# Local attention stack on one core: scores as products over two whole heads, queries moved across partitions by DMA

## Chip, core and metric
One core of a Trainium2 chip runs the whole kernel. The metric is the device time of one execution in microseconds. PE is TensorE, DVE is VectorE, ACT is ScalarE, POOL is GpSimd, and SP is SyncE, which in this kernel issues every DMA. Where a view says SPq, DVEq or PEq, it means that engine's sequencer: what it issues or signals, as distinct from its arithmetic.

## What is computed
The program is a small transformer on x of shape (8, 512, 128): layer norm and attention with 16 heads of 8, then a stack of six layers of local attention with feed-forward, then a second attention block and a gated mix. The change is in the stack. Cut to what matters, one layer of it does this:

```python
q, k, v = split(x @ Wqkv)                 # 16 heads of 64, n = 512 positions
q = rope(l2norm(q) * qs) * scale
k = rope(l2norm(k) * ks) / scale
# windows of 32 positions; each window of queries sees its own and the previous window of keys
sim  = einsum('bhwie,bhwje->bhwij', q_windows, k_two_windows) * 8.0    # 32 x 64 per head and window
attn = softmax(where(mask, -max, sim))
out  = einsum('bhwij,bhwje->bhwie', attn, v_two_windows) @ Wo
x = out + x
x = geglu_ffn(layernorm(x)) + x
```

## The kernel before
Features lie on the 128 partitions and positions along the free axis. `local_stack` walks over 6 layers and, inside a layer, over the 8 sequences of the batch (`body`); a body has four units, `for c in range(NC)`, one for each group of four heads. That makes 6 x 8 x 4 = 192 units. All five engines run the same nest in their own order, and only semaphores tie them together. It is a software pipeline: in unit c the engines project the queries and keys of group c (PE L1021 and L1034), form sums of squares (L1047) and values (L1062), and at the same time work on earlier groups: the scores of group c-2 (L1070 to L1074), the normalised queries and keys `qn` and `kn` of group c-1 (DVE L954), and the product of probabilities with values of group c-3 (PE L1112). Unit c=2 also holds six products with Wo (L1011), and unit c=3 the residual, the layer norm and the feed-forward.

One half of each head lies in `qn[:, 0, :]` and the other in `qn[:, 1, :]`: head r of the group has 32 of its 64 dimensions on partitions 32r to 32r+31 of either half. Keys must not mix between heads when all 128 partitions are contracted, so the keys go by DMA into a block-diagonal tile: `kbd[i]` has four blocks of columns, one per head, and block r is zero outside the partitions of head r. SP issues eight DMAs per unit for that (L775), 32 partitions by 512 positions each:

```python
sp.wait_ge(S["kn_ready"], seen.next(S["kn_ready"]))
...
sp.dma_start(kbd[i][q, r, WIN:KC], kn[q, i, :]).then_inc(S["kbd_full"], 16)
```

The scores of one window are then two products, one per half, with 32 columns of queries as the stationary operand and 4 heads x 64 keys = 256 moving columns; the second accumulates onto the first. A product in float32 shows as two matmul records in the trace, so a unit has 2 banks x 16 products x 2 = 64 records of L1074. The additive mask enters each of the two PSUM banks first, as one bfloat16 product with an identity (L1070).

After the scores, DVE takes the row maximum (L941, tile `l_smax`), subtracts it (L943), later sums and inverts, POOL normalises (L801), and DVE transposes the probabilities in blocks of 32 (L903, tile `l_pt`). SP copies the result into the band `pbd` with eight more DMAs (L764, L767, L768). Before DVE may overwrite `pt`, it waits for `pt_free`, which SP gives at L759 in its own order, after the DMA issues of the unit before:

```python
sp.wait_ge(S["pbd_free"], seen.next(S["pbd_free"]))
sp.sem_inc(S["pt_free"], 1)
sp.wait_ge(S["pt_ready"], seen.next(S["pt_ready"]))
```

DVE's order in a unit is: rotation of the queries (L890), read of the sums of squares (L926), transpose (L903), inverse square root (L87 to L96), rotation of the keys (L890), maximum and subtraction (L941, L943), `qn`, `kn` (L954), sum and reciprocal (L959, L961). PE's order is L1021, L1034, L1047, L1062, scores, broadcast of the norms (L1085, needs the inverse square root), L1112. L1021 of the next unit needs the PSUM tile that L954 reads, so it starts when `kn` is done (semaphore at L956).

Of the kernel before, what the change touches and what calls it, by code (L numbers as in the profile page):

```python
# [15 lines left out]
D = 128  # L16
NB = 8
T = 512
# [16 lines left out]
WIN = 32  # L35
NC = 4
CH = H // NC
KC = T + WIN
# [610 lines left out]
def local_stack(nc, C, xs, A):  # L649
# [8 lines left out]
    with ExitStack() as ctx:  # L658
        def sb(n, shape, dt=F32):
            return ctx.enter_context(nc.sbuf_tensor(f"l_{n}", shape, dt))  # L660
# [18 lines left out]
        kbd = [sb(f"kbd{i}", [D, CH, KC]) for i in range(2)]  # L679
# [22 lines left out]
                 "qn_ready kn_ready kbd_full s_ready t_ready p_ready rec_ready pn_ready pt_ready pt_free pbd_free "  # L702
                 "va_ready pv_ready ot_ready wo_ready x_ready mean_ready centred fsq_ready bc_ready xng_ready "
                 "xnf_ready g_ready a_ready gelu_ready h_ready f_ready ffn_done step pstep init mask_full").split()
        S = {n: sem(n) for n in names}
# [24 lines left out]
        def _(sp):  # L730
# [18 lines left out]
            def body(par, l, start, b, prev):  # L749
# [6 lines left out]
                for c in range(NC):  # L756
# [13 lines left out]
                    if live(c, 1, b, prev):  # L770
                        sp.wait_ge(S["kn_ready"], seen.next(S["kn_ready"]))
                        for i in range(2):
                            for r in range(CH):
                                q = slice(32 * r, 32 * r + 32)
                                sp.dma_start(kbd[i][q, r, WIN:KC], kn[q, i, :]).then_inc(S["kbd_full"], 16)  # L775
# [209 lines left out]
        def _(pe):  # L985
# [5 lines left out]
            def body(par, l, start, b, prev):  # L991
# [23 lines left out]
                for c in range(NC):  # L1015
# [49 lines left out]
                    if live(c, 2, b, prev):  # L1065
                        claim(3, "r3_dve")
                        pe.wait_ge(S["qn_ready"], seen.next(S["qn_ready"]))
                        pe.wait_ge(S["kbd_full"], seen.next(S["kbd_full"], 2 * CH * 16))
                        for bank in range(2):
                            nc.tensor.matmul(R[3][:, bank, :], ident16[:], mask[:, bank, :], start=True, stop=False, skip_group_check=True)  # L1070
                            for w in range(8):
                                W, q = 8 * bank + w, 32 * (w % 4)
                                for half in range(2):
                                    last = nc.tensor.matmul(R[3][q:q + 32, bank, 256 * (w // 4):256 * (w // 4) + 256],  # L1074
                                                            qn[:, half, WIN * W:WIN * W + WIN], kbd[half][:, :, WIN * W:WIN * W + 2 * WIN],
                                                            start=False, stop=(half == 1), skip_group_check=True)
                        last.then_inc(S["s_ready"], 1)
# [333 lines left out]
```

## Time and profile before

| what | value |
|---|---|
| three runs | 5783.74, 5786.65, 5801.6 us; median 5786.65 us |
| profiled execution | 5801.78 us, of which the span of its instructions is 5800.0 us |
| granted TensorE clock, mean | 0.929 of full speed |
| the stack, from its first scores to its last | 738 to 4906 us of the span |
| PE, DVE, ACT, POOL busy | 86%, 71%, 38%, 34% of the span |

Busy shares average over stages with different limits: attention passes at either end, the stack in the middle. A matmul's end is modelled, so consecutive ones overlap and a busy PE need not be at its peak. The view of waits counts only idle time directly before an instruction and names the last thing that released it. The trace does not count DMA issue as busy time of SP, but it shows each issue with its start and duration.

### The profile page before, as it was taken

How to read it: one execution, taken by the hardware profiler on the slowest of the kernel's cores; microseconds unless marked ns; L12 is line 12 of the kernel's file. 1: busy time of each engine (PE TensorE's matmuls, PEld its weight loads, DVE VectorE, ACT ScalarE, POOL GpSimd, SP SyncE). 2: the span in 40 equal slices, each digit the busy share in tenths (PEclk: the TensorE clock that was granted, in tenths of full speed). 3: DMA queues.
4: the chain of work that ended last, by engine and by line, in shares of the span. 5: the costliest groups of instructions: out<-in, count | busy, mean ns of one | idle time of the engine just before them, and what ended most of it. 6: DMA issues, size and time to landing. Idle time of an engine off the chain costs nothing. (4 is left out here: it accounts for less than half of the span.)

```text
span 5800.0 us, 90682 instructions
## 1 busy us (share of the span) xinstructions
PE 4979.5 (86%) x33904; PEld 2765.5 (48%) x34096; DVE 4089.1 (71%) x5868; ACT 2198.8 (38%) x2794; POOL 2000.6 (34%) x1547
## 2 busy tenths in 40 slices
PE   5999688898998999998898998998898998478886
PEld 2222255555555555555555555555555554222223
DVE  4677377777777777777777777777777776366652
ACT  0666333333333333333333333333333332035564
POOL 1111144444444444444444444444444442111110
PEclk6999799999999999999999999999999999579997
DMA  2222111112211122111222112112121111122210
GB/s 58 49 47 44 55 46 48 46 46 61 55 46 49 48 58 58 45 47 47 63 49 49 46 48 69 45 48 50 43 58 48 45 49 47 43 45 45 43 26 16
DMA packets 181029, 279.66 MB, mean 48 GB/s; under 512 B 58032, under 2 KB 79792, under 8 KB 174896
## 3 DMA queue, kind: packets, MB, share of 16 engines
q1 hardware_dynamic: 180880, 277.66, 19.5%
q8 instruction: 94, 1.54, 0.1%
q14 instruction: 55, 0.45, 0.0%
HBM read 61.70 MB, written 17.56 MB: 14 GB/s over the span
## 5 line engine op out<-in xcount | busy, mean ns | idle before, releaser
L792 POOL TENSOR_TENSOR l_u<-l_t 128x512 f32<-128x512 f32 x384 | 486.9, 1268 | 2110.3 <-DVE l_t L890 2110.3
L890 DVE SCALAR_TENSOR_TENSOR l_t<-l_r,l_qkvec,l_tab 128x1024 f32<-128x1024 f32 x768 | 949.3, 1278 | 294.5 <-ACT l_sq L821 291.3
L470 DVE TENSOR_REDUCE a_nmax<-a_pair 128x2 f32<-128x1024 f32 x512 | 612.4, 1221 | 374.5 <-PE a_pair L550 372.5
L1074 PE MATMUL l_r<-l_kbd,l_qn 128*32 128x256 f32 x12288 | 774.5, 390 | 44.5 <-DMA l_kbd<-l_kn 11.3
L388 ACT ACTIVATE a_pt<-a_st 128x512 f32<-128x512 f32 x1024 | 579.8, 597 | 335.4 <-PE a_st L534 325.3
L1021 PE MATMUL l_r<-xs,l_wqkv 128*128 (+1 forms) x768 | 431.9, 690 | 222.4 <-DVEq L956 189.0
L1074 PEld LDWEIGHTS l_r<-l_kbd,l_qn 128*32 128x32 f32 x12288 | 422.9, 111 | 302.2 <-issue 152.8
L1112 PE MATMUL l_r<-l_pbd,l_va 128*64 128x160 f32 (+1 forms) x6144 | 443.4, 297 | 127.7 <-DMA l_pbd<-l_pt 127.7
L534 PE MATMUL a_st<-a_qs,a_ks 75*128 75x512 bf16 x1024 | 391.7, 398 | 146.0 <-ACT a_pt L388 75.5
L801 POOL TENSOR_TENSOR l_p<-l_p,l_srec 128x1024 f32<-128x1024 f32 x192 | 365.3, 1903 | 415.6 <-DVE l_srec L961 284.7
L1112 PEld LDWEIGHTS l_r<-l_pbd,l_va 128*64 128x64 f32 x6144 | 400.2, 138 | 193.1 <-DVEq L896 108.3
L793 POOL TENSOR_TENSOR l_u<-l_t 128x512 f32<-128x512 f32 x384 | 489.2, 1274 | 0.0
L842 ACT ACTIVATE l_p<-l_p 128x1024 f32<-128x1024 f32 x192 | 203.1, 1058 | 721.5 <-DVE l_p L943 721.5
L1062 PE MATMUL l_r<-l_wqkv,l_xc 128*128 128x256 f32 x1536 | 424.7, 425 | 0.0
L1047 PEld LDWEIGHTS l_r<-l_block,l_sqs 128*128 128x128 f32 x3072 | 372.8, 192 | 97.7 <-issue 94.9
L550 PE MATMUL a_pair<-a_ks,a_qs 72*128 72x512 bf16 x1024 | 341.3, 419 | 83.0 <-DMA a_qs<-a_scr 59.7
L829 ACT ACTIVATE l_va<-l_r 128x1024 f32<-128x1024 f32 x192 | 196.7, 1024 | 546.0 <-PE l_r L1062 546.0
L821 ACT ACTIVATE l_sq<-l_r 128x1024 f32<-128x1024 f32 x192 | 196.6, 1024 | 538.3 <-PE l_r L1021 529.9
L1034 PE MATMUL l_r<-xs,l_wqkv 128*128 (+1 forms) x768 | 396.7, 642 | 3.0 <-DVEq L896 2.7
L534 PEld LDWEIGHTS a_st<-a_qs,a_ks 75*128 75x128 bf16 x1024 | 95.5, 97 | 561.1 <-ACT a_pt L388 429.0
L1047 PE MATMUL l_r<-l_block,l_sqs 128*128 128x4 f32 x3072 | 354.1, 247 | 1.4 <-POOL l_sqs L795 1.3
L834 ACT ACTIVATE l_rnx<-l_rn 128x1024 f32<-128x1024 f32 x192 | 203.3, 1059 | 380.5 <-DVE l_rn L96 380.5
(183 smaller groups left out, 7475.3 us busy)
## 6 DMA issues: line engine op xcount, KB each, us to landing
l_kbd<-l_kn SPq DMA_DIRECT2D x1536, 64.0 KB, 2.0
l_pbd<-l_pt SPq DMA_DIRECT2D x1344, 64.0 KB, 2.0
a_ks<-a_scr SPq DMA_DIRECT2D x96, 192.0 KB
a_qs<-a_scr SPq DMA_DIRECT2D x288, 64.0 KB
a_scr<-a_parts SPq DMA_DIRECT2D x48, 256.0 KB, 2.5
l_wqkv<-in_wqkv SPq DMA_DIRECT2D x6, 1536.0 KB, 6.9
l_pbd<-l_pt SPq DMA_DIRECT2D x192, 48.0 KB, 1.9
l_wo<-in_wo SPq DMA_DIRECT2D x6, 512.0 KB, 3.7
```

The costliest lines, as they stand in the source:

```text
L388: nc.scalar.activation(pt[n % 2][:, r, :], st[r % 2][:], ACT.Exp, scale=SC).then_inc(exp_done, 1)
L470: nc.vector.tensor_reduce(out=nmax[:, n, 2 * i:2 * i + 2], in_=pair[i][:], op=ALU.max, axis=AX.X, negate=True).then_inc(pair_dve[i], 1)
L534: nc.tensor.matmul(st[r % 2][:], ks[1 - par][0:ROWS, h, 128 * kt:128 * kt + 128], qs[1 - par][0:ROWS, h, :], start=True, stop=True).then_i ...
L792: nc.gpsimd.tensor_tensor(u[buf][:, 2 * a, :], t[:, 0, :], t[:, 3, :], ALU.subtract)
L793: nc.gpsimd.tensor_tensor(u[buf][:, 2 * a + 1, :], t[:, 2, :], t[:, 1, :], ALU.add).then_inc(S["ra_ready"], 1)
L890: last = nc.vector.scalar_tensor_tensor(out=t[:, 2 * half:2 * half + 2, :], in0=R[a][:, half, :].unsqueeze(1).to_broadcast([D, 2, T]), sca ...
L1021: last = nc.tensor.matmul(R[0][:, half, :], wqkv[par][:, o:o + D], xs[:, b, 0:T], start=True, stop=True)
L1034: last = nc.tensor.matmul(R[1][:, half, :], wqkv[par][:, o:o + D], xs[:, b, 0:T], start=True, stop=True)
L1047: last = nc.tensor.matmul(R[3][:, 0, o:o + CH], sqs[a][:, 128 * k:128 * k + 128], block4[:], start=True, stop=True)
L1062: last = nc.tensor.matmul(R[2][:, k // 2, 256 * (k % 2):256 * (k % 2) + 256], xc[:, 128 * k:128 * k + 128], wqkv[par][:, o:o + CH * DH], s ...
L1074: last = nc.tensor.matmul(R[3][q:q + 32, bank, 256 * (w // 4):256 * (w // 4) + 256], qn[:, half, WIN * W:WIN * W + WIN], kbd[half][:, :, W ...
L1112: last = nc.tensor.matmul(R[1][q:q + 64, bank, 128 * g:128 * g + WIN * span], va[cc][:, g, DH * h:DH * h + DH], pbd[c % 2][:, 0:span, o:o ...
```

## The change
The scores now contract two whole heads at once. For this both dimension halves of a head must lie on different partitions of the same tile. A new tile `qp` takes the queries: head r goes to partitions 64(r mod 2) + 32i for half i, in plane r // 2. `kbd` is laid out in the same way: `kbd[pair]` has two blocks of columns for two heads. A product for one window and one pair of heads contracts 128 partitions and has 2 x 64 = 128 moving columns, and no second product accumulates onto it. The number of products stays at 16 per bank; the order now goes through the four windows inside a pair, so that neighbours write different groups of 32 output partitions. DVE still writes `qn`; eight DMAs per unit copy it into `qp` (SP, L776 of the new program), issued ahead of the eight for `kbd` (L781), and PE waits for `qp_full` where it waited for `qn_ready`. The `kbd` tiles are half as large.

```diff
--- before.py
+++ after.py
@@ -676,7 +676,8 @@
         sq = [sb(f"sq{a}", [D, 2, T]) for a in range(2)]
         sqs = [sb(f"sqs{a}", [D, T]) for a in range(2)]
         qn, kn = sb("qn", [D, 2, T]), sb("kn", [D, 2, T])
-        kbd = [sb(f"kbd{i}", [D, CH, KC]) for i in range(2)]
+        qp = sb("qp", [D, 2, T])
+        kbd = [sb(f"kbd{i}", [D, 2, KC]) for i in range(2)]
         norm = sb("norm", [D, NT * 2 * CH + NT])
         ntmp = sb("ntmp", [D, NT * 2 * CH + NT])
         rn = sb("rn", [D, NT * 2 * CH + NT])
@@ -699,7 +700,7 @@
 
         names = ("late_pe late_act late_dve late_free wqkv_free qkvec_free consts_pe consts_dve xc_ready q_dve q_act k_dve k_act v_act sq_free "
                  "r2_act r0_dve r1_dve r3_dve rq_ready ra_ready sq_sum ss_ready norm_read rn_ready rnx_ready b_ready r0_dve_b "
-                 "qn_ready kn_ready kbd_full s_ready t_ready p_ready rec_ready pn_ready pt_ready pt_free pbd_free "
+                 "qn_ready kn_ready kbd_full qp_full s_ready t_ready p_ready rec_ready pn_ready pt_ready pt_free pbd_free "
                  "va_ready pv_ready ot_ready wo_ready x_ready mean_ready centred fsq_ready bc_ready xng_ready "
                  "xnf_ready g_ready a_ready gelu_ready h_ready f_ready ffn_done step pstep init mask_full").split()
         S = {n: sem(n) for n in names}
@@ -768,11 +769,16 @@
                         sp.dma_start(band[96:128, NT, 0:(NT - 1) * CH * WIN],
                                      turned[0:32, 0, CH:, :].rearrange("p u i -> p (u i)")).then_inc(pbd_full[c % 2], 16)
                     if live(c, 1, b, prev):
+                        sp.wait_ge(S["qn_ready"], seen.next(S["qn_ready"]))
+                        for i in range(2):
+                            for r in range(CH):
+                                q, o = slice(32 * r, 32 * r + 32), 64 * (r % 2) + 32 * i
+                                sp.dma_start(qp[o:o + 32, r // 2, :], qn[q, i, :]).then_inc(S["qp_full"], 16)
                         sp.wait_ge(S["kn_ready"], seen.next(S["kn_ready"]))
                         for i in range(2):
                             for r in range(CH):
-                                q = slice(32 * r, 32 * r + 32)
-                                sp.dma_start(kbd[i][q, r, WIN:KC], kn[q, i, :]).then_inc(S["kbd_full"], 16)
+                                q, o = slice(32 * r, 32 * r + 32), 64 * (r % 2) + 32 * i
+                                sp.dma_start(kbd[r // 2][o:o + 32, r % 2, WIN:KC], kn[q, i, :]).then_inc(S["kbd_full"], 16)
                 if start and prev is not None:
                     sp.wait_ge(S["late_free"], seen.next(S["late_free"]))
                     load_late(l)
@@ -1064,16 +1070,17 @@
                         last.then_inc(S["v_act"], 1)
                     if live(c, 2, b, prev):
                         claim(3, "r3_dve")
-                        pe.wait_ge(S["qn_ready"], seen.next(S["qn_ready"]))
+                        pe.wait_ge(S["qp_full"], seen.next(S["qp_full"], 2 * CH * 16))
                         pe.wait_ge(S["kbd_full"], seen.next(S["kbd_full"], 2 * CH * 16))
                         for bank in range(2):
                             nc.tensor.matmul(R[3][:, bank, :], ident16[:], mask[:, bank, :], start=True, stop=False, skip_group_check=True)
-                            for w in range(8):
-                                W, q = 8 * bank + w, 32 * (w % 4)
-                                for half in range(2):
-                                    last = nc.tensor.matmul(R[3][q:q + 32, bank, 256 * (w // 4):256 * (w // 4) + 256],
-                                                            qn[:, half, WIN * W:WIN * W + WIN], kbd[half][:, :, WIN * W:WIN * W + 2 * WIN],
-                                                            start=False, stop=(half == 1), skip_group_check=True)
+                            for g in range(2):
+                                for pair in range(2):
+                                    for w in range(4):
+                                        W, o = 8 * bank + 4 * g + w, 256 * g + 128 * pair
+                                        last = nc.tensor.matmul(R[3][32 * w:32 * w + 32, bank, o:o + 128],
+                                                                qp[:, pair, WIN * W:WIN * W + WIN], kbd[pair][:, :, WIN * W:WIN * W + 2 * WIN],
+                                                                start=False, stop=True, skip_group_check=True)
                         last.then_inc(S["s_ready"], 1)
                     if has_ss or has_var:
                         pe.wait_ge(S["rnx_ready"], seen.next(S["rnx_ready"]))
```

SP in the steady loop, one unit of the program before: eight issues for the band (`l_pbd`), then eight for the keys (`l_kbd`).

```order
L764 DMA l_pbd<-l_pt 32x512 [waits l_pbd_free,l_pt_ready]
L764 DMA l_pbd<-l_pt 32x512 x3
L767 DMA l_pbd<-l_pt 32x512 x3
L768 DMA l_pbd<-l_pt 32x384
L775 DMA l_kbd<-l_kn 32x512 [waits l_kn_ready]
L775 DMA l_kbd<-l_kn 32x512 x7
L764 DMA l_pbd<-l_pt 32x512 [waits l_pbd_free,l_pt_ready]
```

The same place in the changed program, whose L765 to L769 are L764 to L768 of the one before:

```order
L765 DMA l_pbd<-l_pt 32x512 [waits l_pbd_free,l_pt_ready]
L765 DMA l_pbd<-l_pt 32x512 x3
L768 DMA l_pbd<-l_pt 32x512 x3
L769 DMA l_pbd<-l_pt 32x384
L776 DMA l_qp<-l_qn 32x512 [waits l_qn_ready]
L776 DMA l_qp<-l_qn 32x512 x7
L781 DMA l_kbd<-l_kn 32x512 [waits l_kn_ready]
L781 DMA l_kbd<-l_kn 32x512 x7
L765 DMA l_pbd<-l_pt 32x512 [waits l_pbd_free,l_pt_ready]
```

Ahead of the eight issues for the keys, eight for `l_qp` have come in, with a wait of their own; a unit issues 24 DMAs where it issued 16, all on SP, and the next `pt_free` stands behind all of them. On DVE, ACT and POOL nothing moves, and on PE the products stay where they were, with half the moving columns.

## Rows read from the trace of the kernel before
**Rows 1.** The page, part 1: engine, busy us, share, instructions.
```profile
span 5800.0 us, 90682 instructions
...
PE 4979.5 (86%) x33904; PEld 2765.5 (48%) x34096; DVE 4089.1 (71%) x5868; ACT 2198.8 (38%) x2794; POOL 2000.6 (34%) x1547
```

**Rows 2.** Windows: length, busy of PE, PEld, DVE, ACT, POOL, clock, DMA share, GB/s.
```profile
2016.37:2034.54 18.17, 14.79 (x138) 10.03 (x139) 15.33 (x23) 6.10 (x6) 9.38 (x7) 1.00 0.23 57
2363.50:2383.11 19.61, 16.42 (x138) 10.62 (x139) 15.31 (x23) 6.11 (x6) 9.37 (x7) 0.91 0.21 53
2054.56:2084.35 29.79, 28.67 (x175) 16.75 (x175) 20.24 (x32) 12.23 (x14) 11.12 (x8) 0.94 0.20 50
738.00:4906.00 4168.00, 3757.80 (x28408) 2335.80 (x28599) 3197.71 (x4855) 1467.99 (x1517) 1780.54 (x1330) 0.96 0.20 50
```

**Rows 3.** Timeline, unit c=1: start us, duration us, engine, line.
```profile
2016.30 4.94 SPq L775 DMA_DIRECT2D l_kbd<-l_kn  x8
...
2016.37 1.99 PE L1021 MATMUL l_r<-xs,l_wqkv 128*128 x4 [2.03 <-DVEq L956]
...
2021.61 1.97 PE L1062 MATMUL l_r<-l_wqkv,l_xc 128*128 128x256 f32 x8
...
2022.53 1.25 DVE L903 STREAM_TRANSPOSE l_pt<-l_p 128x1024 f32<-128x1024 f32 x1 [0.21 <-DVE l_norm L926]
...
2023.73 1.97 PE L1074 MATMUL l_r<-l_kbd,l_qn 128*32 128x256 f32 x32
2023.81 2.41 SPq L764 DMA_DIRECT2D l_pbd<-l_pt  x4
...
2025.95 1.97 PE L1074 MATMUL l_r<-l_kbd,l_qn 128*32 128x256 f32 x32
...
2026.79 2.47 DVE L890 SCALAR_TENSOR_TENSOR l_t<-l_r,l_qkvec,l_tab 128x1024 f32<-128x1024 f32 x2
2026.90 1.06 ACT L834 ACTIVATE l_rnx<-l_rn 128x1024 f32<-128x1024 f32 x1 [2.26 <-DVE l_rn L96]
...
2028.01 1.09 PE L1085 MATMUL l_r<-ident,l_rnx 128*128 128x128 f32 x8
...
2029.39 1.23 DVE L941 TENSOR_REDUCE l_smax<-l_r 128x16 f32<-128x1024 f32 x1
...
2032.09 1.22 DVE L954 TENSOR_TENSOR l_qn<-l_u,l_r 128x1024 f32<-128x1024 f32 x1 [0.21 <-POOL l_u L793]
...
2033.22 1.21 DVE L954 TENSOR_TENSOR l_kn<-l_u,l_r 128x1024 f32<-128x1024 f32 x1
2034.46 1.78 SPq L775 DMA_DIRECT2D l_kbd<-l_kn  x3
```

**Rows 4.** The tile l_smax: idle of its engine before it, until what.
```profile
  PE l_r L1074: 8.8, 2
```

**Rows 5.** The tile l_pt: the transposes, and idle before them.
```profile
L903 DVE STREAM_TRANSPOSE l_pt<-l_p x192: 1245/1245/1247, 756.6 to 4913.5; 128x1024 f32<-128x1024 f32 x192
...
  SPq L759: 4.6, 4
```

**Rows 6.** Timeline about a slow batch of DMA issues.
```profile
2897.21 6.45 SPq L775 DMA_DIRECT2D l_kbd<-l_kn  x8
...
2903.76 1.25 DVE L903 STREAM_TRANSPOSE l_pt<-l_p 128x1024 f32<-128x1024 f32 x1 [0.53 <-SPq L759]
```

**Rows 7.** The tile l_kbd: its DMA issues, and their time to landing.
```profile
L775 SPq DMA_DIRECT2D l_kbd<-l_kn x1536: 507/591/2097, 729.0 to 4898.1; - x192
...
DMA to landing us min/median/max: 1.9/2.0/3.6
```

**Rows 8.** Timeline, scores partly at the lower clock.
```profile
2327.76 2.90 PE L1074 MATMUL l_r<-l_kbd,l_qn 128*32 128x256 f32 x32 [0.36 <-issue]
```

**Rows 9.** Timeline, end of a unit c=2.
```profile
2047.10 5.32 PE L1011 MATMUL l_r<-l_ot,l_wo 128*128 128x512 f32 x12
```

**Rows 10.** The view of waits: the feed-forward on PE.
```profile
PE l_r L1125 <- ACT l_xc L845: 38.4, 44, 1.6
```

## Prediction
> **What bounds the kernel now.** I read the page first. PE is busy 86% of the span and DVE 71% [rows 1], which suggests that fewer columns on PE should pay. That is a mean over stages, so the next view is the windows by unit. A plain unit c=1 takes 18.17 us, of which PE works 14.79 and DVE 15.33; a unit c=3 takes 29.79 with PE busy 28.67 [rows 2]. In c=1 neither engine is full, so something circulates. The timeline of that unit shows what [rows 3]. DVE ends `kn` at 2034.43 and PE's L1021 of the next unit follows at once; DVE waits for its result through ACT, rotates, transposes (L903, 2022.53 in the unit shown), takes the inverse square root, rotates the keys until 2029.26, and starts the row maximum at 2029.39, directly behind. From the transpose's start to the end of `qn` (2033.31) DVE hardly pauses: 10.78 us.
>
> Where are the scores in this? They end near 2027.9 (the second bank starts at 2025.95 and lasts 1.97), and DVE is not ready for them before 2029.26. The view of the tile `l_smax` says it for the whole run: DVE waited for a score product 2 times in 192, 8.8 us in all [rows 4]. In steady units the scores are off the path.
>
> The second thing to read is SP. Its eight issues for the keys take 4.94 us [rows 3] at a median of 591 ns each [rows 7], so the pitch is (4.94 - 0.59)/7 = 0.621 us. They run from 2016.30 to 2021.24, and only then does SP give `pt_free`, 1.3 us ahead of the transpose at 2022.53. How thin this margin is shows where a batch of issues was slow: it ended at 2903.66, and the transpose started at 2903.76 with SP named as its releaser [rows 6]. That happened 4 times, for 4.6 us [rows 5].
>
> **Part 1: half the columns.** A bank's 32 records come as eight steps of four records, which write different groups of 32 output partitions, and take 1.97 us [rows 3]; less the tail of the last record (0.39) and the small offsets that is near 0.216 us per step of 256 columns. The nearest row with 128 columns is L1085: eight records in 1.09 us, or (1.09 - 0.27)/7 = about 0.115. I take a step as halved. That saves 8 x 0.108 = 0.87 us per bank, 1.75 per unit, 336 us of PE work over 192 units. The other bound is nothing saved: the number of records and of weight loads is unchanged, and no row has 32-column products this short. I take the halving, because L1085 loads four times as many weight columns and still keeps that rate. On the path the saving is worth nothing in c=0, 1 and 2, where DVE starts the maximum later than the scores end. In c=3 PE looks full, but its feed-forward waits for ACT's L845 in nearly every body [rows 10], behind the same DVE chain. Value on the path: 0, covered by the rotation of the keys (L890 until 2029.26, a margin of 1.3 us).
>
> **Part 2: eight more issues on SP.** The new batch for `qp` starts when `qn` is ready, 1.1 us before `kn`, and the keys' eight follow it. I price an issue as one for the keys: same 32 partitions by 512 positions, 64 KB. That the destination lies on other partitions is not new, since the band's L767 does so. The minimum of 507 ns and the slowest batch of 6.45 us are the bounds. Sixteen issues take 15 x 0.621 + 0.59 = 9.91 us. The band's issues, begun at 2023.81, are long over when `qn` ends. So there is a new circle, and every term of it has a row:
>
> - transpose start to end of `qn`: 10.78 us [rows 3]
> - `qn` to SP's first issue: 0.03, as from `kn` (2034.43) to its issue (2034.46) [rows 3]
> - sixteen issues: 9.91 [rows 3, 7]
> - end of the last issue to the next transpose: 0.10 [rows 6]
>
> Sum: 20.82 us from transpose to transpose, against 18.17 in the warm unit and 19.61 in one where the granted clock had a stretch at 1.2 GHz [rows 2]. From all 192 starts of L903, of which rows 5 gives the first and the last, I worked out the intervals of 47 bodies. The means are 18.74 us from c=0 to c=1 and 18.95 from c=1 to c=2, then 24.48 to c=3 and 25.15 on to the next c=0. The last two exceed the circle (in c=3 `qn` ends 11.2 us after the transpose, which makes 21.2), so the extra issues hide there, with at least 3.6 us to spare. The first two don't: 47 x (20.82 - 18.74) + 47 x (20.82 - 18.95) = 97.8 + 87.9 = **+185.7 us**.
>
> **Part 3: the new wait of PE.** PE stands at the scores until the last key copy has landed. That issue starts 0.69 us before the transpose and lands 2.0 later [rows 7], 1.3 us after the transpose's start, where scores began 0.7 to 1.2 after it before. Behind this wait in PE's order are L1085, the output products L1011 and the band product. With the saving of part 1 the scores, mask included, take about 2.95 us and end 4.3 us after the transpose. L1085 can't start before ACT's `rnx`, at 2027.96 - 2022.53 = 5.43 [rows 3], and DVE wants them at 6.7. Margin 1.1 us: cost 0 at full clock. But PE now idles ahead of the scores: L1062 (2021.61, 1.97 us) ends 1.1 us after the old transpose time, which the new one passes by 2.65, so the keys land about 2.9 us later than that end. In these traces an idle stretch ahead of work went with a lower clock behind it: the c=1 unit from 2363.50 has 0.91 and is 1.44 us longer [rows 2]. In c=0 to c=1 to c=2 the queue's circle covers that. In c=2 it doesn't: there L1011 (5.32 us, [rows 9]) and c=3 follow PE densely. A bank of scores partly at 1.2 GHz took 2.90 in place of 1.97 [rows 8], so I expect 1 to 3 us more for both, less the margin. Taken as 0.8 us in half of the 47 bodies: **+18 us**, between 0 and some 90.
>
> **The rest.** Next to layer loads and at the ends of the stack batches ran slower, up to 6.45 us for eight. I put 1 us on some eight of them: **+8 us**. The smaller memset of `kbd` gains a microsecond or two, which I leave out.
>
> **Sum.** 5801.8 (the profiled execution) + 185.7 + 18 + 8 = 6013.5; I say **6013 us**. The profiled execution lies 15 us above the median of 5786.65. I correct nothing for it, since the two intervals that change would be set by SP's queue whatever the clock did before.
>
> The Trainium skill, "DMA: Bandwidth & Descriptors", section "Issuing engines are not separate DMA queues", calls the sequencer time to start a DMA usually small relative to the DMA itself. The trace here disagrees: 0.6 us of issue stands against 2.0 us to landing, and sixteen in a row take 9.9 us. By that rule the extra copies would vanish and the sum would stay near 5800.
>
> **Rivals.**
>
> *PE sets the unit, and the saving shows (faster).* Place: the scores in every unit; price: 192 x 1.75 = 336 us off, 5466 us. It decides if DVE's maximum waits for the scores in most units and SP keeps ahead. For it speaks the 86%; against it rows 4 and the circle above. Chance 0.03.
>
> *The issues hide (no change).* The new copies start 1.1 us earlier and the queue is busy with two batches of 4.94, so 9.9 of 18.2 us. Sixteen would have to end before 2022.5, that is in 7.3 us, or 0.46 us each; the lowest issue in the trace is 507 ns. About 5800 us. Chance 0.04.
>
> *The products don't get shorter.* Then the scores end 6.05 us after the transpose, 0.6 past `rnx`. In c=1 and c=2 the circle still covers it, in c=2 to c=3 it costs 47 x 0.6 = 28 us more: about 6041, and more where the clock falls. For it speaks that 64 records now take about 4.2 us with a mean near 62 ns, which could be a rate of records rather than of columns. Against it: records inside a step start closer than that. Chance 0.10. The Trainium skill, "TensorE: Matmul & The Clock Gate", section "Wait — 56ns, not 53.3ns?", has a rule to this effect: without hardware decode the sequencer spends about 62 ns per matmul, which binds once the array work is shorter. By it 64 records would need 4.0 us whatever their columns; the trace can't yet tell.
>
> *The queue is slower under a third more issues.* At the pitch of the slow batch, 6.45/8 = 0.8 us, sixteen take 12.7 and the circle is 23.6: +260 more, 6280 us. Only a handful of 192 batches were like that, each near other loads. At half that excess it is 6140. Chance 0.06.
>
> **Numbers.** The forecast has 0.77: SP's circle binds c=1 and c=2 only. The range of 5965 to 6095 takes in a pitch 5% off (0.5 us in 94 units, 47 us), no clock loss, up to 80 us of it, and the third rival. What a measurement can tell from no change is about 0.3%, or 17 us. Slower 0.93, same 0.04, faster 0.03.
>
> **What would show it.** In the new profile the transpose waits for SP (the semaphore line ahead of the band's issues) some 94 times for about 2.5 us each; starts of transposes in c=0 to c=2 lie 20.8 us apart and the others stay at 24.5 and 25.1; a bank of scores lasts near 1.1 us; the maximum still waits for scores rarely. I am wrong if intervals stay near 18.2, if c=3 grows too, if sixteen issues don't take 9.9 us, or if PE's projections rather than SP release the transpose.

## The result and the profile after

The changed kernel takes 5996.98 us (median of 4 runs, 5977.96 to 6024.16) against 5785.19 (4 runs, 5779.81 to 5801.6): a ratio of 1.0365, 95% interval 1.0318 to 1.0411. The forecast was 6013, range 5965 to 6095. The profiled execution took 5991.18 us, its granted clock is 0.89 where it was 0.929.

The page of the changed kernel, its span, part 1 and the group of the scores; then windows of one unit c=1 and of the stack (length, busy of PE, PEld, DVE, ACT, POOL, clock, DMA share, GB/s). They answer to [rows 1, 2].

```profile
span 5989.4 us, 92268 instructions
...
PE 4801.1 (80%) x33904; PEld 2818.8 (47%) x34096; DVE 4029.9 (67%) x5868; ACT 2207.3 (37%) x2794; POOL 1998.9 (33%) x1547
...
L1081 PE MATMUL l_r<-l_kbd,l_qp 128*32 128x128 f32 x12288 | 545.4, 333 | 369.8 <-DMA l_kbd<-l_kn 350.4
```

```profile
2617.00:2638.00 21.00, 15.36 (x137) 11.19 (x138) 14.56 (x24) 6.22 (x6) 9.36 (x7) 0.84 0.31 76
741.60:5110.90 4369.30, 3597.29 (x28336) 2402.05 (x28526) 3130.76 (x4838) 1473.47 (x1514) 1770.54 (x1323) 0.90 0.29 71
```

PE works 178 us less and the kernel is 212 us longer. No engine got fuller: each waits longer for something else. What it is stands in the tiles `l_pt`, `l_smax`, `l_qp` and `l_kbd` (as [rows 4, 5, 7]).

```profile
L909 DVE STREAM_TRANSPOSE l_pt<-l_p x192: 1245/1245/1247, 741.6 to 5110.9; 128x1024 f32<-128x1024 f32 x192
...
  SPq L760: 281.4, 98
...
  PE l_r L1081: 36.5, 66
...
L776 SPq DMA_DIRECT2D l_qp<-l_qn x1536: 507/591/1847, 710.6 to 5092.0; - x192
...
L781 SPq DMA_DIRECT2D l_kbd<-l_kn x1536: 577/590/1689, 715.7 to 5097.1; - x192
...
DMA to landing us min/median/max: 2.0/2.0/3.3
```

The transpose waits for SP's `pt_free` 98 times and 281.4 us, where it was 4 times and 4.6 us [rows 5]. The copies cost what the key copies cost [rows 7]. The timeline of that unit c=1 and the start of c=2 (start us, duration us, engine, line), for [rows 3]:

```profile
2617.53 1.25 DVE L909 STREAM_TRANSPOSE l_pt<-l_p 128x1024 f32<-128x1024 f32 x1 [2.95 <-SPq L760]
...
2619.53 1.94 PE L1081 MATMUL l_r<-l_kbd,l_qp 128*32 128x128 f32 x32 [3.69 <-DMA l_kbd<-l_kn]
...
2623.80 1.66 PE L1092 MATMUL l_r<-ident,l_rnx 128*128 128x128 f32 x8
2623.94 1.23 DVE L947 TENSOR_REDUCE l_smax<-l_r 128x16 f32<-128x1024 f32 x1 [0.46 <-PE l_r L1081]
...
2626.63 1.22 DVE L960 TENSOR_TENSOR l_qn<-l_u,l_r 128x1024 f32<-128x1024 f32 x1 [0.21 <-issue]
...
2627.88 4.95 SPq L776 DMA_DIRECT2D l_qp<-l_qn  x8
...
2632.87 5.02 SPq L781 DMA_DIRECT2D l_kbd<-l_kn  x8
...
2636.00 1.26 POOL L799 TENSOR_TENSOR l_u<-l_t 128x512 f32<-128x512 f32 x1
...
2637.98 1.25 DVE L909 STREAM_TRANSPOSE l_pt<-l_p 128x1024 f32<-128x1024 f32 x1 [2.95 <-SPq L760]
2639.15 0.14 DVE L87 TENSOR_SCALAR l_ntmp<-l_norm 128x32 int32<-128x32 int32 x1
...
2645.76 5.32 PE L1017 MATMUL l_r<-l_ot,l_wo 128*128 128x512 f32 x12
```

The circle of the prediction (a chain of waits that comes back to its own start once per unit, so that its length bounds the interval) can be walked: `qn` ends at 2627.85, sixteen issues run from 2627.88 to 2637.89, the next transpose starts 0.09 later. Two things in it were not forecast in this form. A bank of scores takes 1.94 us here, not 1.1; PE stood still for 3.69 us ahead of it, and the granted clock is low there (question C tests that). And L87, the first step of the inverse square root, takes 0.14 us. It took 0.92 in the kernel before, where it ran beside POOL:

```profile
2023.30 1.28 POOL L793 TENSOR_TENSOR l_u<-l_t 128x512 f32<-128x512 f32 x1
...
2023.70 0.92 DVE L87 TENSOR_SCALAR l_ntmp<-l_norm 128x32 int32<-128x32 int32 x1
```

From the 192 starts of the transpose I worked out the mean intervals of 47 bodies, as the prediction did. "Low" counts the stretches of the lower granted clock inside the stack.

| kernel | c3 to c0 | c0 to c1 | c1 to c2 | c2 to c3 | all, us | low |
|---|---|---|---|---|---|---|
| before | 25.15 | 18.74 | 18.95 | 24.48 | 4104 | 91 |
| after | 25.19 | 20.91 | 20.40 | 25.30 | 4315 | 177 |
| forecast | 25.15 | 20.82 | 20.82 | 24.86 | 4307 (+8) | |

In us over the 47 bodies the four changes are +1.8, +102.0, +68.3 and +38.6, together 211. The profiled executions differ by only 189, as 15 us more lay ahead of the first transpose of the stack in the old one (756.6 against 741.6) and 8 more behind the last.

### The profile page after: what moved, and what is told of

The parts are those of the page before. It is cut to its first block and busy times, and to the rows that moved or that the text cites. A ratio compares the mean times of both kernels' runs of the same rounds, so it can differ in the third digit from the quotient of the medians.

```text
span 5989.4 us, 92268 instructions
## 1 busy us (share of the span) xinstructions
PE 4801.1 (80%) x33904; PEld 2818.8 (47%) x34096; DVE 4029.9 (67%) x5868; ACT 2207.3 (37%) x2794; POOL 1998.9 (33%) x1547
## 5 line engine op out<-in xcount | busy, mean ns | idle before, releaser
L1081 PE MATMUL l_r<-l_kbd,l_qp 128*32 128x128 f32 x12288 | 545.4, 333 | 369.8 <-DMA l_kbd<-l_kn 350.4
L1119 PE MATMUL l_r<-l_pbd,l_va 128*64 128x160 f32 (+1 forms) x6144 | 509.8, 326 | 136.3 <-DMA l_pbd<-l_pt 136.3
L1119 PEld LDWEIGHTS l_r<-l_pbd,l_va 128*64 128x64 f32 x6144 | 465.9, 154 | 202.2 <-issue 151.4
L1027 PE MATMUL l_r<-xs,l_wqkv 128*128 (+1 forms) x768 | 391.0, 632 | 128.5 <-DVEq L962 97.6
L799 POOL TENSOR_TENSOR l_u<-l_t 128x512 f32<-128x512 f32 x384 | 487.5, 1270 | 0.0
L1081 PEld LDWEIGHTS l_r<-l_kbd,l_qp 128*32 128x32 f32 x12288 | 399.8, 133 | 167.4 <-issue 152.8
L1068 PE MATMUL l_r<-l_wqkv,l_xc 128*128 128x256 f32 x1536 | 445.5, 441 | 0.0
L909 DVE STREAM_TRANSPOSE l_pt<-l_p 128x1024 f32<-128x1024 f32 x192 | 239.1, 1245 | 303.8 <-SPq L760 281.4
L1040 PE MATMUL l_r<-xs,l_wqkv 128*128 (+1 forms) x768 | 369.6, 604 | 3.2 <-DVEq L902 3.2
```

Source lines behind the costliest of these rows:

```text
L799: nc.gpsimd.tensor_tensor(u[buf][:, 2 * a + 1, :], t[:, 2, :], t[:, 1, :], ALU.add).then_inc(S["ra_ready"], 1)
L1027: last = nc.tensor.matmul(R[0][:, half, :], wqkv[par][:, o:o + D], xs[:, b, 0:T], start=True, stop=True)
L1040: last = nc.tensor.matmul(R[1][:, half, :], wqkv[par][:, o:o + D], xs[:, b, 0:T], start=True, stop=True)
L1068: last = nc.tensor.matmul(R[2][:, k // 2, 256 * (k % 2):256 * (k % 2) + 256], xc[:, 128 * k:128 * k + 128], wqkv[par][:, o:o + CH * DH], s ...
L1081: last = nc.tensor.matmul(R[3][32 * w:32 * w + 32, bank, o:o + 128], qp[:, pair, WIN * W:WIN * W + WIN], kbd[pair][:, :, WIN * W:WIN * W + ...
L1119: last = nc.tensor.matmul(R[1][q:q + 64, bank, 128 * g:128 * g + WIN * span], va[cc][:, g, DH * h:DH * h + DH], pbd[c % 2][:, 0:span, o:o ...
```

## Experiments

Four questions: does SP's circle set the time, and per issue or per byte (A); what are the halved columns worth (B); what does the lower clock cost (C); is there a kernel faster than both (D)? Ratios are against the kernel before, run beside each. Its median was 5785 us beside the changed kernel and 5789 to 5799 beside the others, so where two variants that ran apart are compared I give the difference of their times and, behind it, that of their excesses over the kernel before.

### A. The circle

**Four copies in place of eight.** If the blocks of queries are laid out as half by pair, two heads move in one copy of 64 partitions, so a unit has 12 issues for `qp` and `kbd` where the change has 16.

```diff
-                            for r in range(CH):
-                                q, o = slice(32 * r, 32 * r + 32), 64 * (r % 2) + 32 * i
-                                sp.dma_start(qp[o:o + 32, r // 2, :], qn[q, i, :]).then_inc(S["qp_full"], 16)
+                            for pair in range(2):
+                                sp.dma_start(qp[64 * i:64 * i + 64, pair, :], qn[64 * pair:64 * pair + 64, i, :]).then_inc(S["qp_full"], 16)
```

> The changed kernel with another order of the four 32-row blocks in a pair, so that the queries need four DMAs of 64 partitions in place of eight of 32; the keys still take eight. Theory (time is counted in issues on SP, 0.62 us each whatever their size): twelve issues take 7.4 us, the circle is 20.82 - 4 x 0.621 = 18.3 us, waits for pt_free shrink to 0.2 us or less, and the time is that of the kernel before, 5785 us within 20. Rival (an issue costs by its partitions or bytes): no change, about 5997 us.

Measured 5731.07 us (5728 to 5740), ratio 0.9889 (0.9868 to 0.9911). The issues in its timeline, then the row of its tile `l_qp` and the landing:

```profile
2498.43 2.42 SPq L775 DMA_DIRECT2D l_qp<-l_qn  x4
```

```profile
L775 SPq DMA_DIRECT2D l_qp<-l_qn x768: 462/597/617, 714.7 to 4827.1; - x192
...
DMA to landing us min/median/max: 2.2/2.4/3.9
```

An issue of 64 partitions and twice the bytes takes 597 ns, where one of 32 takes 591. The interval from c=0 to c=1 is 18.36 to 18.39 in steady bodies. The loss is gone, and the kernel is 68 us faster than the kernel before beside it, which I had not expected: question B.

**Four issues more.** Four copies of `qn` into a tile that nothing reads, between the two batches. PE waits for them too.

```diff
+                        for r in range(CH):
+                            sp.dma_start(qx[32 * r:32 * r + 32, :], qn[32 * r:32 * r + 32, 0, :]).then_inc(S["qp_full"], 16)
```

> The changed kernel with four more DMAs on SP between queries and keys, which copy 32 partitions of qn each into a tile that nothing reads; PE waits for them too. Theory (the circle is counted in issues, 0.62 us each): it grows from 20.9 to 23.4 us in c=0 to c=1 and c=1 to c=2, 94 units x 2.5 = 233 us, about 6230 us; the transpose waits for SP about 5.4 us each time. From c=2 to c=3 nothing or little. Rival (the queue has slack and only the landing counts): under 6100 us.

Measured 6236.01 us (6227 to 6239), ratio 1.0756 (1.0719 to 1.0794). The idle time before the transpose there, and its batches in one unit:

```profile
  SPq L760: 519.2, 107
```

```profile
3312.07 4.95 SPq L776 DMA_DIRECT2D l_qp<-l_qn  x8
3317.07 2.48 SPq L778 DMA_DIRECT2D l_qx<-l_qn  x4
3319.59 5.02 SPq L783 DMA_DIRECT2D l_kbd<-l_kn  x8
```

From 12 to 16 to 20 issues the interval goes 18.36, 20.89, 23.42 us: 2.53 for each four, 0.63 per issue. So the wait behind a row of issues on one queue is what the change costs; bytes and partitions per copy do not show in it.

**The release moved ahead.** The issues stay, but SP gives `pt_free` for the next unit after the band's issues, ahead of the waits for `qn` and `kn`.

```diff
-                        sp.wait_ge(S["pbd_free"], seen.next(S["pbd_free"]))
-                        sp.sem_inc(S["pt_free"], 1)
+                        if c == 0:
+                            sp.wait_ge(S["pbd_free"], seen.next(S["pbd_free"]))
+                            sp.sem_inc(S["pt_free"], 1)
...
+                    if c < NC - 1 and live(c + 1, 3, b, prev):
+                        sp.wait_ge(S["pbd_free"], seen.next(S["pbd_free"]))
+                        sp.sem_inc(S["pt_free"], 1)
                     if live(c, 1, b, prev):
                         sp.wait_ge(S["qn_ready"], seen.next(S["qn_ready"]))
```

> The changed kernel, but SP gives pt_free for units c=1, 2 and 3 one step earlier, ahead of the sixteen issues for queries and keys. Theory (the circle closes through pt_free and SP's issues): the transposes of c=1 and c=2 no longer wait for SP; what waits next is PE at the scores, whose keys land 11.4 us after the end of qn. With scores at the higher clock (2.9 us) a unit is about 18.3 us, with scores at the lower clock (about 4.7 us, as the changed kernel's profile shows in many units) about 20.2. So between 5760 and 5930 us; I take 5900, because the idle stretch ahead of the scores stays. Rival (the landing of the keys on PE is an equal bound, pt_free only looks like one): above 5960 us.

Measured 5972.85 us (5957 to 5999), ratio 1.0314 (1.0276 to 1.0352): the rival was right, and of some 210 us 24 came back (38 by the excesses). The transpose no longer waits for SP; what waits now is the row maximum, for the scores (idle us, times):

```profile
  SPq L761: 0.7, 2
...
  PE l_r L1085: 182.3, 81
```

Its unit c=2 reads so:

```profile
4080.75 4.94 SPq L780 DMA_DIRECT2D l_qp<-l_qn  x8
...
4085.74 5.02 SPq L785 DMA_DIRECT2D l_kbd<-l_kn  x8
...
4092.86 1.94 PE L1085 MATMUL l_r<-l_kbd,l_qp 128*32 128x128 f32 x32 [3.69 <-DMA l_kbd<-l_kn]
...
4095.27 1.94 PE L1085 MATMUL l_r<-l_kbd,l_qp 128*32 128x128 f32 x32
...
4097.27 1.22 DVE L951 TENSOR_REDUCE l_smax<-l_r 128x16 f32<-128x1024 f32 x1 [2.45 <-PE l_r L1085]
...
4101.21 4.95 SPq L780 DMA_DIRECT2D l_qp<-l_qn  x8
```

From one batch for `qp` to the next (4080.75 to 4101.21) are 20.46 us: ten of issues, 1.6 until PE goes on, two banks at the lower clock, the maximum, the subtraction and `qn`. That is a second circle through the same queue, and the interval of 20.44 to 20.46 us that 31 of 47 bodies of the changed kernel show from c=1 to c=2 is this one. Counted from one `qn` to the next instead of by transposes, both kernels have a median of 20.45 us from c=0 to c=1 and from c=1 to c=2. The release does move the transpose: the mean interval from c=0 to c=1 falls from 20.91 to 18.37 us (119 us over the bodies), but the one from c=2 to c=3 grows from 25.30 to 27.44 (101 us, up to 28.6 in one body). Taking one circle away left the other.

### B. The halved columns

**Old products, new copies.** The kernel before, with the eight `qp` copies and PE's wait for them; its products still read `qn`.

```diff
+                        sp.wait_ge(S["qn_ready"], seen.next(S["qn_ready"]))
+                        for i in range(2):
+                            for r in range(CH):
+                                q, o = slice(32 * r, 32 * r + 32), 64 * (r % 2) + 32 * i
+                                sp.dma_start(qp[o:o + 32, r // 2, :], qn[q, i, :]).then_inc(S["qp_full"], 16)
...
-                        pe.wait_ge(S["qn_ready"], seen.next(S["qn_ready"]))
+                        pe.wait_ge(S["qp_full"], seen.next(S["qp_full"], 2 * CH * 16))
```

> The kernel before, with the eight query copies of the change issued on SP ahead of the keys and waited for by PE, but with the old products of 256 columns, which read qn. Theory: the circle of 20.9 us stands as in the changed kernel, and the longer scores (1.75 us more at the higher clock, 3.5 at the lower) push L1085 and what follows from c=2 to c=3 back by 1.2 to 2.5 us per body: 6050 to 6110 us, 6070 likeliest, with DVE's maximum waiting for scores in many units. Rival (the shorter products are worth nothing even now): 5997 us.

Measured 6040.17 us (6029 to 6059), ratio 1.0413 (1.0392 to 1.0435), slightly under the expected range. Its maximum waits for the scores so:

```profile
  PE l_r L1080: 107.6, 61
```

With the copies there, the halving is worth 6040 less 5997, 43 us (30 by the excesses).

**New products, no copies.** The change without its copies; the products read `qn` in its old layout, so the scores contract the wrong rows and only the time of this kernel counts.

```diff
-                                                                qp[:, pair, WIN * W:WIN * W + WIN], kbd[pair][:, :, WIN * W:WIN * W + 2 * WIN],
+                                                                qn[:, pair, WIN * W:WIN * W + WIN], kbd[pair][:, :, WIN * W:WIN * W + 2 * WIN],
```

> The changed kernel without the query copies: the new products of 128 columns read qn in place of qp, so the scores contract the wrong rows; everything else is computed. Theory (scores are off the path while the keys land in time): 5785 us within 20, as the kernel before, although PE works some 300 us less. Rival (PE's columns bound the kernel): up to 336 us faster, 5450 us. Second rival (the emptier PE runs at the lower clock more often): 20 to 60 us slower than before.

Measured 5744.9 us (5739 to 5755), ratio 0.9912 (0.989 to 0.9934): 54 us under the kernel before beside it, so less than the expected 5785, and far from the 5450 of the rival on PE's columns. The saving of 336 us of PE is worth a sixth of that in time.

The 54 us of this kernel and the 68 of the one with four copies are not the scores getting off the path; they never were on it [rows 4]. The kernel before loses time elsewhere: in 18 of 47 bodies the interval from c=0 to c=1, and in 27 that from c=1 to c=2, is 19.5 to 19.9 us in place of 18.15. Two windows of it, and then L1021 and L1034 in the first of them:

```profile
3418.10:3423.40 5.30, 5.23 (x8) 2.21 (x9) 2.15 (x3) 1.02 (x1) 1.90 (x1) 0.68 0.35 86
3437.70:3442.90 5.20, 5.17 (x8) 2.19 (x9) 3.00 (x4) 1.02 (x1) 1.90 (x1) 0.67 0.36 87
```

```profile
3418.17 3.39 PE L1021 MATMUL l_r<-xs,l_wqkv 128*128 x4 [2.02 <-DVEq L956]
3421.36 2.21 PE L1034 MATMUL l_r<-xs,l_wqkv 128*128 x4
```

A granted clock of 0.68 is a stretch at 1.2 and the rest at 2.4 GHz. PE had idled 2.02 us ahead of L1021, 1.99 us long at the full clock, and it is on the circle of DVE. 45 such intervals at 1.4 us are 63 us. The idle time alone does not decide it: of the 92 units of c=1 and c=2 whose L1021 waited for DVE, 45 ran at a lowered clock and 47 at the full one, and the wait was about 2.0 us in most of either kind ([rows 3] has one of 2.03 at the full clock). What decides, no run here shows.

**PE kept busy there.** The kernel before, with six products of the mask into a bank that is written afresh later, ahead of the projections of c=1 and c=2.

```diff
+                    if c in (1, 2) and b is not None and prev is not None:
+                        read(3)
+                        for _ in range(6):
+                            nc.tensor.matmul(R[3][:, 0, :], ident16[:], mask[:, 0, :], start=True, stop=True, skip_group_check=True)
```

> The kernel before with six extra mask products (1.3 us) on PE in units c=1 and c=2, after the band product and ahead of L1021's wait, where PE idles 2 us. Theory (the kernel before loses 1.4 us per body wherever L1021 falls to the lower clock; shorter scores in e2 and e4 only moved the low stretches to work with slack): the intervals c=0 to c=1 and c=1 to c=2 return to 18.15 us from means of 18.74 and 18.95: about 65 us off, 5725 us. Rival (the gain of e2 and e4 is PE work saved): 5787 us, or slower by the fillers.

Measured 5732.95 us (5725 to 5742), ratio 0.9882 (0.9845 to 0.9919). The clock in the same place:

```profile
3397.60:3402.80 5.20, 5.17 (x24) 3.24 (x24) 3.50 (x4) 2.05 (x2) 1.90 (x1) 1.00 0.36 87
```

All intervals from c=0 to c=1 but two or three are 18.15 now. Adding work that nobody reads to the old kernel gives what four copies and halved columns give together. That argues for the clock as the source of most of the gain there too, though no run isolates it: the traces with four copies and with none have more low stretches in the stack (105 and 124 against 91), but only 11 and 8 intervals above 19 us from c=0 to c=2 where the kernel before has 45. The low stretches have moved to the band product, which has slack: in the units after the transposes of c=0 and c=1 it takes 2.8 us and more, in place of 2.29, 58 and 76 times, against twice in the kernel before. With four copies 17 us of the gain lie from c=2 to c=3, and most of that is another effect (question D).

### C. The lower clock in the changed kernel

Twelve such products ahead of the scores of c=1 and c=2, where PE idled.

```diff
+                        if c in (1, 2):
+                            for _ in range(12):
+                                nc.tensor.matmul(R[3][:, 0, :], ident16[:], mask[:, 0, :], start=True, stop=True, skip_group_check=True)
```

> The changed kernel with twelve extra mask products (bfloat16, 512 columns, 2.6 us in all) on PE in units c=1 and c=2, between the claim of the scores' PSUM tile and the wait for queries and keys; what they write is overwritten by the mask. Theory (idle ahead of the scores is what lowers the clock, and scores at 1.2 GHz cost only from c=2 to c=3): a bank of scores in c=2 falls from 1.94 to 1.08 us, c=2 to c=3 from a mean of 25.3 to about 24.4, the two intervals before it stay at 20.9 and 20.1 to 20.4: 47 x 0.9 = 42 us less, about 5955 us. Rival (the longer c=2 to c=3 comes from the late keys, not from the clock): 5997 us or, with the fillers in the way, more.

Measured 5910.89 us (5908 to 5921), ratio 1.0198 (1.0161 to 1.0235): 86 us below the changed kernel (96 by the excesses), twice what I expected. PE in its timeline, then the windows of the scores in it and in the changed kernel:

```profile
2614.88 2.54 PE L1075 MATMUL l_r<-l_mask,l_ident 128*128 128x512 bf16 x11
2618.01 0.38 PE L1079 MATMUL l_r<-l_mask,l_ident 128*128 128x512 bf16 x1 [0.59 <-DMA l_kbd<-l_kn]
2618.31 1.08 PE L1084 MATMUL l_r<-l_kbd,l_qp 128*32 128x128 f32 x32
...
2619.65 1.08 PE L1084 MATMUL l_r<-l_kbd,l_qp 128*32 128x128 f32 x32
2621.21 1.09 PE L1095 MATMUL l_r<-ident,l_rnx 128*128 128x128 f32 x8 [0.48 <-ACT l_rnx L840]
2622.14 3.17 PE L1017 MATMUL l_r<-l_ot,l_wo 128*128 128x512 f32 x7
```

```profile
2617.90:2622.10 4.20, 3.61 (x74) 2.71 (x75) 3.89 (x12) 1.06 (x1) 0.00 (x0) 1.00 0.32 78
```

```profile
2639.40:2645.70 6.30, 5.71 (x73) 4.43 (x75) 5.49 (x14) 1.06 (x1) 1.69 (x2) 0.52 0.33 81
```

At full clock both banks, their masks and L1095 are over at 2622.3, 4.3 us after the first mask product began; in the changed kernel (clock 0.52) they run from 2639.4 to 2645.9, 6.5 us, and L1017 starts later by as much. Its interval from c=2 to c=3 goes from 25.30 to 23.62 (79 us over the bodies), that from c=1 to c=2 from 20.40 to 20.16 (11 us). The row maximum waits for scores 3 times, 6.9 us in all. The interval from c=0 to c=1 stays at 20.89: the queue's circle does not care for the clock.

A bank of 32 records in 1.08 us also settles the rival on records. The Trainium skill, "TensorE: Matmul & The Clock Gate", section "Wait — 56ns, not 53.3ns?", gives about 62 ns per matmul as the bound once the array work is shorter and hardware decode is off. By that rule a bank would take 2 us. The trace shows 1.08 us, 34 ns per record, so the bound does not hold here; which way of decoding was in use, no trace shows.

### D. Together

The kernel with four copies plus the early release:

> Queries in four DMAs (as e2_qp_in_four) and pt_free given one step earlier (as e1_early_ptfree). Theory: with twelve issues the circle of 18.3 us is only just the longest; without it c=0 to c=1 falls from 18.36 to the 18.15 us of the DVE chain: 47 x 0.2 = 10 us off 5731, 5721 us within 15. Rival (the two edits add up, early pt_free is worth the 24 us it brought in e1): 5707 us. If the keys' landing were the bound instead, no change from 5731.

Measured 5730.12 us (5721 to 5748), ratio 0.9877 (0.984 to 0.9914), the same as with four copies alone. The transpose had still waited for SP with four copies (41.9 us over 81 times). Without that the steady interval from c=0 to c=1 went from 18.36 to 18.15, but the one from c=2 to c=3 from 24.15 to 24.38: with the transpose earlier, L87 in c=2 has a median of 0.90 us where it had 0.68.

That kernel with the six products ahead of the projections added, and the one with four copies and the same six:

> Queries in four DMAs, pt_free one step earlier, and six extra mask products on PE ahead of L1021 in c=1 and c=2. Theory (the halved columns save nothing on the path, what they brought in e2 and e4 was that low-clock stretches fell on work with slack): with L1021 kept at the higher clock all bodies take 85.7 us, as in e10: 5725 us, the same as e10 within 10. Rival (PE work saved counts by itself): 20 us or more below e10.

> As e9 without the earlier pt_free. The transpose in c=1 and c=2 then starts about 0.2 us later, behind SP, and the first step of the inverse square root (L87), which in every profile so far ends 0.04 us after POOL's product L793 of the old numbering, starts later but ends at the same time. Theory: nothing lost by the later transpose from c=1 to c=3, 0.2 us lost once from c=0 to c=1: equal to e9 within 10 us. Rival (pt_free's wait is paid in full): 94 x 0.2 = 19 us above e9.

Measured 5757.33 us (5745 to 5770), 0.9956 (0.9941 to 0.9971), and 5774.92 us (5756 to 5796), 0.9986 (0.997 to 1.0001). Both expectations on size were wrong: what helps the old kernel harms this one. (What the second expectation's rival gave for the second over the first, 19 us, is near the 18 measured.) The trace of the first shows how. PE, and a window of it:

```profile
4760.56 1.09 PE L1099 MATMUL l_r<-ident,l_rnx 128*128 128x128 f32 x8 [1.86 <-ACT l_rnx L843]
4762.76 4.32 PE L1126 MATMUL l_r<-l_pbd,l_va 128*64 128x160 f32 x32 [1.11 <-DMA l_pbd<-l_pt]
4767.02 2.21 PE L1029 MATMUL l_r<-l_mask,l_ident 128*128 128x512 bf16 x6
```

```profile
4762.70:4769.00 6.30, 6.24 (x38) 4.75 (x39) 5.51 (x6) 2.08 (x2) 4.45 (x5) 0.54 0.27 64
```

The short scores leave PE idle twice, 1.86 and 1.11 us, ahead of the band product L1126, which then runs at the lower clock (4.32 us where it is 2.29 elsewhere), and so do the extra products, behind which the projections of the next unit stand: the interval here is 20.02 us. With the old products the scores fill the first of the two gaps, and behind the second alone (1.13 us in the kernel before) the band product keeps its 2.29 us: it was slow in 2 of 96 such units in the old kernel with the same six products, and in 57 of 96 here. Over the stack the intervals sum to 4074 us in the one kernel and 4089 in the other, against 4040 to 4051 in those with fill or four copies alone. Why the second is 18 us above the first stays open. The wait for `pt_free` is back (29.2 us over 51 times), but with four copies alone that wait cost nothing against the kernel with the early release (5731 and 5730); and there are more low stretches (94 against 81), the trace does not show why.

So the old kernel with extra products (5733) and the changed one with four copies (5731) are the best, about 1% below the kernel before. Both ran again:

> The kernel before with six extra mask products ahead of L1021 once more, beside e9 on the same chip: 5730 us within 10.

> Queries in four DMAs once more, on the same chip as e9: 5731 us within 10, of which the extra products of e11 would take off 5 to 20, since some bodies still have a low-clock L1021.

Measured 5733.26 us (5722 to 5741), 0.9906 (0.989 to 0.9923), and 5731.8 us (5718 to 5746), 0.9917 (0.9901 to 0.9933).

## Why the prediction was right

The forecast of 6013 lies 16 us above the result, within its range, and its mechanism is the one that runs. By its steps:

- **The circle through SP** (part 2). Forecast 20.82 us from c=0 to c=1; measured 20.89, with 10.01 us for the sixteen issues in place of 9.91. 98 waits of the transpose for 281 us, forecast some 94 of 2.5; their median is 2.95. The slope of 0.63 us per issue, shown with 12, 16 and 20 issues, is the pitch of 0.621 from [rows 7]. Right, and shown. What it lacked is the second circle, through the landing of the keys, the scores and `qn`: at the lower clock it takes 20.45 us and sets 31 of the 47 intervals from c=1 to c=2, and for its sake an earlier `pt_free` wins little (question A).
- **10.78 us from transpose to `qn`** was taken as fixed. It isn't: from c=1 to c=2 and on to c=3 the delayed transpose comes after POOL's L799 has ended, and L87 takes 0.14 us, not 0.92. So the circle of SP is 20.12 there. At the clock of question C's kernel the two intervals have means of 20.16 and 23.62 us, where the forecast without its clock term had 20.82 and 24.48: 47 x (0.66 + 0.86) = 71 us less. That L87 is the reason is read from traces; no run was made for it alone.
- **The clock** (part 3), +18 us between 0 and 90, is the term that was mis-sized: the kernel of question C gets 86 us back, and its two intervals from c=1 to c=3 alone 90. I had the mechanism (PE idles ahead of the scores) and gave it 0.8 us in half the bodies. It is 1.7 us on the mean of all of them from c=2 to c=3 (about 2.1 in 32 of the 47), because each product behind the idle time runs at the lower level, mask products and L1092 too. The row maximum waits for scores 66 times, where I wrote rarely.
- These two errors cancel, and that is luck: 71 us too many, and some 70 too few (90 against 18). A right total doesn't show right terms; the intervals do.
- **The halving** (part 1): 0.87 us a bank was forecast, and at full clock a bank goes from 1.97 to 1.08, 0.89. PE's busy time fell by 178 us only, not 336, since much of it ran at the lower clock. That the halving is worth nothing on the path holds for the scores themselves at the old timing. But with no copies it gives 54 us, most likely through the clock on L1021, and with all eight copies 30 to 43, where I saw nothing to gain. My sum kept those 60 us lost to the clock in the kernel before as if they were its work.
- **The sum.** I corrected nothing for the 15 us by which the profiled execution lay above its median, arguing from the clock inside the stack. In the two traces the old kernel has 15 us more ahead of the stack than the new one; whether its other executions lack them, no trace shows. Median to median the change is 211.8 us; the terms summed to 211.7, and 5785 + 212 is 5997.
- The rivals fell: PE sets the unit (5466, decided by c=1's 20.9), the issues hide (4.95 + 5.02 us don't), the products don't get shorter (1.08 us a bank), the queue slows under more issues (pitch unchanged at 20 issues).

## What to carry to other kernels

Count the DMA issues between a producer and the next semaphore that the same queue gives: each cost its pitch on the circle here, 0.63 us with 32 partitions as with 64, so merge copies before you move their order, and look for the next circle through the same queue before you expect the release alone to help. Before you price a saving, list the intervals of a unit over all bodies: those longer than the rest point to the clock, and a change of timing anywhere ahead of them can win or lose more than the work it removes. Test such a kernel with a few products that nobody reads, but again after every other edit, since the idle time moves.

## What the hardware showed

- L87, a tensor_scalar of 32 columns on DVE, when it starts beside POOL's running product on `l_u`, ends 0.038 us after that one ends (0.034 to 0.045 in all but a few cases, 0.129 at most). Overlapped it took 0.5 to 0.9 us in most cases, alone 0.14 to 0.17. In the kernel before it met that product 187 times of 193, in the changed one 95. The Trainium skill, "SBUF — State Buffer", section "Who interferes with whom", says that a tensor_scalar on VectorE in its two-port mode and GpSimd share a port pair as an exclusive lock, and that the one that comes second waits until the other ends. The trace agrees, 0.92 us against 0.14; that L87 runs in this mode, no run shows.
- Copies between partitions cost SP 0.59 to 0.60 us each to issue, with 32 or with 64 partitions, and land 2.0 or 2.4 us after issue.
- PE idle for 2 to 3.7 us was followed in many units by stretches whose granted clock was 0.52 to 0.68, but after about 2.0 us also by the full clock, in half of the cases ahead of L1021 of the kernel before; products issued in that idle time kept it at 1.00 in two kernels, and in two others moved the lower stretch to the band product and to themselves.
